# Linear attention and a feed-forward layer on one core: thirteen products of zeros at the start taken out

## The reference

```python
h = layernorm(x)
q, k, v, gate = h @ Wq.T, h @ Wk.T, h @ Wv.T, h @ Wg.T       # 8 heads of 16
q, k = rope(q), rope(k)
kv, ksum, vsum = einsum('bshd,bshe->bhde', k, v), k.sum(1), v.sum(1)
num = einsum('bshd,bhde->bshe', q, kv) * scale + vsum
den = einsum('bshd,bhd->bsh', q, ksum) * scale + S
o = num / den + conv5(v, lepe_w, lepe_b)                      # depthwise, along the sequence
x = x + (o * gate) @ Wo.T
h2 = layernorm(x)                                             # then in bf16
y = dot(fp8(h2 / s_in), fp8(kernel / s_k)) * (s_in * s_k)
return x + y + bias
```

## Time and profile before

| | us |
|---|---|
| three runs | 168.59, 168.31, 168.03 |
| median | 168.31 |
| the profiled execution | 168.34 |
| its span, first to last instruction | 166.5 |
| busy in it: PE / DVE / POOL / ACT | 151.6 / 149.7 / 133.9 / 125.6 |
| PE's instructions | 1047 products, as many weight loads |
| mean granted clock of PE by the records | 0.984 |

### The profile page before, as it was taken

One profiled execution on the slowest core, in us unless ns is written; L12 is line 12 of the kernel. 1 busy time (PEld: TensorE's weight loads), 2 busy tenths in 40 slices (PEclk: granted clock), 3 DMA queues, 4 the chain that ended last, 5 costly groups with the idle time before them and its releaser, 6 DMA issues.

```text
span 166.5 us, 3671 instructions
## 1 busy us (share of the span) xinstructions
PE 151.6 (91%) x1047; PEld 122.7 (74%) x1047; DVE 149.7 (90%) x279; ACT 125.6 (75%) x342; POOL 133.9 (80%) x162
## 2 busy tenths in 40 slices
PE   7599989999999999999999999999999999998530
PEld 2176888896868888888979786898978788875410
DVE  1368999989989999999999999999999999999583
ACT  4769791666997889788898998856698887666931
POOL 1456898784989799989999989968879797998850
PEclk9999999999999999999999999999999999999985
DMA  4931520210151617252736132227122423104113
GB/s 140 274 122 41 128 63 17 52 32 4 33 126 32 195 32 210 76 138 65 216 127 164 56 100 63 65 45 238 35 77 58 96 76 84 31 4 157 65 63 126
DMA packets 16390, 15.51 MB, mean 93 GB/s; under 512 B 8944, under 2 KB 10352, under 8 KB 16368
## 3 DMA queue, kind: packets, MB, share of 16 engines
q1 hardware_dynamic: 15936, 14.99, 32.9%
q10 hardware_dynamic: 432, 0.26, 0.6%
HBM read 5.02 MB, written 4.19 MB: 55 GB/s over the span
## 4 chain that ended last, share of the span: by engine, by line
PE 56%; DVE 17%; issue 11%; ACT 7%; POOL 6%; DMA 2%; DVEq 1%; ACTq 0%; POOLq 0%
PE bank L1276 6%; PE bank L1302 6%; PE p_num L1321 6%; DVE acc L981 6%; PE p_num L1313 6%; PE bank L1266 6%; PE bank L1340 6%; PE bank L1257 5%; PE bank L1284 5%; PE bank L1249 4%; PE bank L1330 3%; PE bank L1292 3%; ACT h L441 2%; POOL rs L661 2%; DMA xs<-in_x_dram 2%
## 5 line engine op out<-in xcount | busy, mean ns | idle before, releaser
L981 DVE SCALAR_TENSOR_TENSOR acc<-bank,columns,acc 128x510 f32<-128x510 f32 (+1 forms) x48 | 34.7, 723 | 0.3 <-ACT outer L413 0.3
L441 ACT ACTIVATE h<-x,nmr,rs 128x128 bf16<-128x128 f32 x60 | 24.7, 483 | 3.8 <-POOL nmr L664 3.3
L383 ACT ACTIVATE h<-xs,nmr,rs 128x128 f32<-128x128 f32 x64 | 26.2, 484 | 0.5 <-POOL nmr L653 0.5
L661 POOL TENSOR_TENSOR rs<-ve,minus_half 128x4 f32<-128x4 f32 (+1 forms) x17 | 16.6, 977 | 10.0 <-ACT ve L432 10.0
L697 POOL TENSOR_TENSOR k<-k_turned 128x512 f32<-128x512 f32 x16 | 20.4, 1274 | 4.5 <-DVE k_turned L966 4.5
L706 POOL TENSOR_TENSOR acc<-acc,outer 128x508 f32<-128x508 f32 x16 | 20.3, 1267 | 2.3 <-DVE acc L981 2.3
L650 POOL TENSOR_TENSOR rs<-ve,minus_half 128x4 f32<-128x4 f32 (+1 forms) x17 | 16.6, 976 | 5.7 <-ACT ve L374 5.6
L966 DVE TENSOR_TENSOR k_turned<-bank,turn_k 128x1024 f32<-128x1024 f32 x16 | 19.5, 1220 | 1.2 <-PE bank L1266 0.9
L690 POOL TENSOR_TENSOR qT<-q_turned,q_swapped 128x512 f32<-128x512 f32 x16 | 20.4, 1274 | 0.1
L954 DVE TENSOR_TENSOR q_turned<-bank,turn_q 128x1024 f32<-128x1024 f32 x16 | 19.5, 1217 | 0.9 <-PE bank L1257 0.7
L1302 PEld LDWEIGHTS bank<-v,k 128*128 128x128 f32 x128 | 16.6, 190 | 4.5 <-issue 3.1
(11 more groups left out here) (81 smaller groups left out, 334.7 us busy)
## 6 DMA issues: line engine op xcount, KB each, us to landing
q_swapped<-q_turned SPq DMA_DIRECT2D x32, 128.0 KB, 2.3
xs<-in_x_dram SPq DMA_DIRECT2D x15, 256.0 KB, 3.3
out_dram<-ob SPq DMA_DIRECT2D x15, 256.0 KB, 2.5
xs<-in_x_dram SPq DMA_DIRECT2D x2, 128.0 KB, 2.9
turn_q<-in_turn_q_dram SPq DMA_DIRECT2D x1, 256.0 KB, 4.5
out_dram<-ob SPq DMA_DIRECT2D x2, 128.0 KB, 2.0
h2T<-h SPq DMA_TRANSPOSE x14, 2.4
w_qk<-in_w_qk_dram ACTq DMA_DIRECT2D x1, 128.0 KB, 2.9
```

The lines of the kernel that those rows point to most:

```text
L383: last = nc.scalar.activation(h[:, s, t], xs[:, u % NX, t], ACT.Identity, scale=rs1[:, s, t:t + 1], bias=nmr1[:, s, t:t + 1])
L441: last = nc.scalar.activation(h2[:, s3, t], x2[:, u % 4, t], ACT.Identity, scale=rs2[:, s, t:t + 1], bias=nmr2[:, s, t:t + 1])
L981: nc.vector.scalar_tensor_tensor(out=part, in0=p_vT[:, :, lo + off:hi + off], scalar=conv_w[:, k:k + 1], in1=part, op0=ALU.mult, op1=ALU.a ...
```

## The change

The buffer `zero`, its memset on DVE, the semaphore `zero_set`, PE's wait for it, the helper `keep_busy` and its one call are removed. Nothing else is moved or altered: PE's first instruction is then the wait for `h` of unit 0's first half.

```diff
--- before.py
+++ after.py
@@ -100,7 +100,6 @@
         qn = sb("qn", [P, W])
         minus_half = sb("minus_half", [P, TPU])
         eps = sb("eps", [P, 1])
-        zero = sb("zero", [P, W], BF16)
         scratch = sb("scratch", [P, 1])
 
         xs = sb("xs", [P, NX, TPU, D])
@@ -174,7 +173,6 @@
         f_in = sem("f_in")
         c_in = sem("c_in")
         ob_free = [sem(f"ob_free{n}") for n in range(3)]
-        zero_set = sem("zero_set")
         scales_done = sem("scales_done")
         w_ready = sem("w_ready")
         rounding = [sem(f"rounding{n}") for n in range(N_ROUNDING)]
@@ -827,7 +825,6 @@
                 ins.then_inc(w_chain, 1)
                 dve.wait_ge(w_chain, links[0])
 
-            nc.vector.memset(zero[:], 0.0).then_inc(zero_set, 1)
             def widen_turn_k():
                 dve.wait_ge(turn_k_in, 16)
                 nc.vector.tensor_copy(turn_k[:].rearrange("p a o (b h f) -> p (a o b) h f", b=2, h=H),
@@ -1231,10 +1228,6 @@
 
         @block.tensor
         def _(pe):
-            def keep_busy(bank_free, times):
-                for _ in range(times):
-                    nc.tensor.matmul(bank_free[:], zero[:, 0:P], zero[:], start=True, stop=True)
-
             def wait_freed(freed):
                 for semaphore, value in freed:
                     pe.wait_ge(semaphore, value)
@@ -1388,8 +1381,6 @@
                 with pe.If(is_small == 0):
                     products(q16)
 
-            pe.wait_ge(zero_set, 1)
-            keep_busy(p_gT, 13)
             transpose_h(0, j=0)
             transpose_h(0, j=1)
             project_q(0)
```

## The result

| | before | changed |
|---|---|---|
| median of four runs, us | 168.20 | 172.16 |
| lowest to highest | 168.03 to 168.59 | 171.41 to 172.68 |
| ratio | | 1.023, 95% interval 1.0197 to 1.0263 |
| the profiled execution, time / span | 168.34 / 166.5 | 172.68 / 170.9 |

The change costs 4.0 us where 1.8 was forecast and 171.3 was the end of the range. The profiled execution is the slowest of the four, and its 4.4 us are taken apart here.

The account below looks back on a forecast made before the run. PE and DVE were read as near full, with PE alone bounding the first dense stretch. Terms 0 + 0 + 0.22 + 1.6 gave +1.8 us on 168.31, so 170.1 us, range 169.0 to 171.3.

Parts of the forecast that it names:

- (1): Start, DVE: removing the memset of `zero` saves 0.27 us of DVE, hidden by the DMA of x; gain nothing.
- (3): Unit 0's four transposes run at the lower clock; first pair covered, second on the chain: +0.22 us.
- Part (5): After the first dense stretch: the delay hits PE and DVE in full; nothing booked back from PE's idle time.
- (D): Not slower: PE's idle time from 13.40 to 50 us takes up the late work; 168.3 to 168.6 us, chance 0.08.
- Part (4): PE's first dense stretch starts at the lower clock, 3.2 us long, half of it lost: +1.6 us.
- rival (B): Late clock rise: PE slow for 4.2 to 5.8 us of dense work, +2.3 to +3.1 us, chance 0.18.
- (A): The forecast itself: a slow dense stretch of 2 to 4.2 us, +1.2 to +2.3 us, chance 0.62.
- Part (2): Start, PE: removing 13 products, their weight loads and the wait frees 4.38 us before first data; nothing gained.
- The last of my own signs of being wrong: In the profile after, waits appear in the middle that the kernel before does not have; no size given.
- Rival (E): Faster: 13 products less to fetch let the first loads go out sooner; 167.8 us at best, chance 0.02.

Follow-up runs that it names:

- the late start with the same number: Six fp32 and one bf16 product of zeros in place of the 13 bf16 ones of the kernel before; 170.65 us, ratio 1.0156.

## Why the prediction was wrong

**What held.** The bound: PE alone bounds the first dense stretch, and the slow step is twice the full one. Parts (1) and (3): the memset costs nothing, a pair of transposes takes 0.25 us more (0.22 forecast). Part (5): the delay goes through the whole pipeline undiminished, 2.9 us at 16 us and 2.8 at 116 us; PE's idle time up to 25 us is the same 0.64 us as it was (8.38 of 9.02 us busy). Rival (D) fell with that.

**Part (4) was a size, and held by the medians.** I took 3.2 us of slow dense work. The changed kernel showed 5.2, 3.2 and about 3.1 us in its three traces by the delay that they left (half of each is the loss), and the five other kernels whose clock was not up in time 4.6 to 6.0. So rival (B)'s length was seen more often than (A)'s, both within one kernel, and one should have been forecast as the spread of the other. By the medians the clock's share is 1.9 us with 13 narrow products in front and 2.3 us with them at unit 10, against my +1.8 for parts (3) and (4). That my sum came this close to it is in part luck: the length had no row. The Trainium skill (TensorE: Matmul & The Clock Gate, Part 1), with under 1% of a typical kernel's span for the ramp, is a little low for this kernel: 1.9 of 168.1 us is 1.1%. Its remark that the number of slow products differs between runs of one kernel is what these traces show.

**Part (2) is the step that failed.** I costed the 13 products and 13 weight loads at nothing because PE is idle where they ran. That counts their time and not their place in the stream. The last of my own signs of being wrong came true: a wait in the middle that the kernel before does not have, 1.28 us at 136.82 us. The packets of q8, 16 KB each, move when PE's stream alone is changed, and with 26 instructions fewer ahead of the work one such packet falls 1.2 us behind the issue of the DMA transpose of unit 10 in each of three traces, where it had come 0.3 us ahead. The transpose lands in 3.8 to 4.2 us instead of 2.5, ACT's quantisation is late, and PE loses 1.1 to 1.4 us with the other engines in tow. By the medians it is 1.6 us (171.61 less 170.06), and 1.0 us by the two kernels that differ only in where the narrow products stand (1.9 us over before in front, 2.9 us at the end, each over its own chip's before). The experiments show this from both sides: the instructions without their work take the loss away, put in front or some 25 us ahead of the place; put behind the last step they don't; and 42 more of them with the clock and the start as in before bring 3.4 us. Rival (E) had the right object, fewer instructions to fetch, and the wrong sign.

The Trainium skill (Runtime: NRT & Kernel Launch, Instruction fetch mechanics) says that an engine's instructions are refilled in blocks of 16 KiB, 256 instructions, over a DMA queue of its own, and that the cost of crossing a block's end is mostly hidden. The nine packets of q8 agree with the first part, 0.15 MB in all. The second holds here for PE, whose only new wait is for ACT, but not for the kernel: the transpose beside the load landed 1.3 to 1.8 us late. Had I counted blocks by this page, I would have seen that 26 is a tenth of a block and that the loads had to move.

**What is not settled.** That the packet and the late landing go together is shown in fourteen traces, and the interventions move both. Which loads move by how much when instructions are taken out, I can't say: with 14 fewer the packet came 5 us later than in the kernel before, where I had reckoned with 0.8, and with the same number, but fp32 products among them, it came 5 us later too. PE's feed-forward step stands twice in its program, each time behind a branch (`pe.If`), so the stream holds code that is jumped over; whether the jumps set where loads fall is untested. And the median of the late start with the same number is 1 us higher than its trace explains.

## What to carry to other kernels

An instruction that does nothing useful is still a place in its engine's stream. Where a kernel has DMAs on its critical path that bear no delay, compare variants of the kernel with the stream kept as it is (keep the instruction, empty its work), or a change of 1% can be the loads of instructions falling elsewhere. An equal count alone did not hold the loads in place when the kind of product was changed, so look in the trace where the packets of the instruction queue fall. And for work ahead of the first data: what it buys is read from the steps between starts, not from the clock row; take more than one trace, since the slow stretch lasted from 3.1 to 5.2 us in three executions of one kernel.

## What the runs showed that I had not expected

A DMA transpose of a 128x512 bf16 tile, 2.4 us in nearly all of its executions, takes 3.6 to 4.2 us when a 16 KB instruction packet starts 1.2 us after its issue (chains of waits of four kernels). The DMA's busy share is 1.02 while only 63 GB/s move: the recorded times of packets overlap, so the share is no measure of what is moved. Columns as in the earlier trace rows:

```profile
132.74:134.70 1.96, 1.96 (x13) 1.44 (x13) 1.75 (x3) 1.68 (x4) 1.96 (x2) 1.00 1.02 63
```

PE's clock fell back between two pieces of work: up at 6.19 us, down at 8.37 us, after zeros that ended near 4.6 us and two pairs of transposes. And five products of 2 columns each, under 0.3 us of PE's time, changed a kernel of 168 us by 2.6 us, by medians on two chips.
